# Transposed input from the host, layer norm folded into centered weights, and a new opening order in a four-stage block

## The chip, the cores and the metric

The kernel runs on one core of one Trainium2 chip. The metric is the device time of one execution in microseconds. Five engines of the core work side by side, each through its own queue of instructions, and meet through semaphores: TensorE (PE; its weight loads are shown apart as PEld), VectorE (DVE), ScalarE (ACT), GpSimd (POOL) and SyncE (SP), which here only starts DMAs.

## The reference

The input `x` has 4 batches of 512 tokens with 512 features. `_layernorm` has no weights: it subtracts the mean over the features and divides by the square root of the variance plus 1e-5.

```python
# _L0_attn_a_ref: a dense layer whose matrix is made here
attn = jnp.einsum('ds,td->st', w1, w2) * sparse_mask
y = jnp.einsum('bds,st->bdt', x, attn) + b2
return jax.nn.gelu(y, approximate=False)
# _L0_ffn_ref
dots = jax.nn.softmax(x @ centroids.T / TEMPERATURE, axis=-1)
hits = dots > THRESHOLD
query_sel, cluster_sel = jnp.any(hits, axis=1), jnp.any(hits, axis=0)
row_sel = cluster_sel[assignments]
dense = x @ weight.T + bias
out = jnp.where(query_sel[:, None] & row_sel[None, :], dense, 0)
...
x = x + _L0_attn_a_ref(_layernorm(x), w1, w2, b2, sparse_mask)      # stage 1
x = x + _L0_ffn_ref(_layernorm(x), weight, bias, centroids, assignments)   # stage 2
x = x + _L0_attn_b_ref(_layernorm(x), Wqkv, bqkv, Wo, bo)           # stage 3: one-head attention
x = x + _L0_ffn_ref(_layernorm(x), weight, bias, centroids, assignments)   # stage 4
```

All of it is float32. `cluster_sel` needs every token of every batch, so stages 2 and 4 each end in a point that all batches must reach.

## The kernel before

The 2048 tokens are 16 tiles of 128 tokens on the partitions (4 batches `b` of 4 tiles `t`, `n = 4b + t`), and `x_tok` holds them in on-chip memory throughout. A product that contracts over features needs its operands with the features on the partitions. So every normalized tile is transposed by TensorE in four 128x128 blocks, into one of four PSUM banks `t_bank` (line 1013). For accuracy each operand is split in two: ScalarE copies it rounded to a `_hi` part (line 719), VectorE subtracts that from the original to get a `_lo` part (line 813), and a product is the three matmuls hi·hi, lo·hi, hi·lo of each of the four 128-feature chunks, 12 matmuls in all (`products`, line 947), into one of four banks `m_bank`.

One tile of stage 1 passes these steps: VectorE's statistics (`stats`, lines 824 and 825), GpSimd's `rstd` and `nbias` (lines 650 to 652), ScalarE's `norm` into `xn_odd` (line 696), TensorE's transpose, the split, the product `y1` with the matrix `attn` and, as a thirteenth matmul, a row of ones times the split bias `b2` (line 951), ScalarE's Gelu straight from PSUM (line 734), and VectorE's residual sum into `x_tok` (step `x1`, line 850). Stage 2 normalizes the new `x_tok` into `xn_even` in the same way, transposes it, and makes two products: the cluster logits `cl2` for a whole batch (line 1048) and the dense `dn2` per tile. ScalarE copies `dn2` to `y_tok` (line 745) and GpSimd adds the bias (`bias_f`, line 661). The logits are transposed back (`tc2`); VectorE sums and subtracts their maximum (lines 905 to 908), ScalarE exponentiates in one instruction of 128x256 (line 784), and VectorE makes the selection (`prob2`, lines 914 to 924). Stage 4 is stage 2 again, with `x4`, `cl4`, `dn4`.

In the opening, `w2` is loaded in four column pieces and transposed by TensorE (16 blocks), `w1` is loaded in rows, and `attn` is built from 48 matmuls into the four `m_bank`s, masked by VectorE (line 836) and split (lines 723 and 840). The FFN weight arrives in the buffer that `w2` has left and is transposed between the tiles of batch 0.

The order is written out by hand. `schedule()` returns one list of steps; each engine walks that list and issues what is its own, so that a step's place in the list is its place in every engine's queue. In the loop over batches 1 to 3 it places the four `y1` products of batch `b` first and then `cl2` and four `dn2` of batch `b - 1`, with the transposes, splits and norms between them.

## Time and profile before

| | |
|---|---|
| median of 3 runs | 318.18 us (317.98 to 318.34) |
| span of the profiled execution | 317.0 us |
| TensorE busy | 285.5 us, 90% |
| VectorE busy | 232.8 us, 73% |
| ScalarE busy | 167.1 us, 53% |
| GpSimd busy | 162.3 us, 51% |

The span runs from the first to the last instruction of one profiled execution; what lies outside it is the rest of the device time. Engines are busy at the same time, so their shares don't add up. A share is a mean over stages. The granted clock of TensorE, given for a stretch, is 1.00 at 2.4 GHz and 0.50 at 1.2 GHz.

### The profile page before, as it was taken

The numbers are of one execution on the slowest core, as the hardware profiler recorded it, in microseconds if no ns is written. First come the engines' busy times: TensorE is split into PE (matmuls) and PEld (weight loads), VectorE is DVE, ScalarE is ACT, GpSimd is POOL, SyncE is SP. The second block draws the span as 40 slices with busy tenths as digits, with TensorE's granted clock in tenths as the row PEclk, the third lists the DMA queues.
The fourth block names the chain that finished last, engine by engine and source line by source line (L and its number), as shares of the span: only waits on it lengthen the run. The fifth ranks groups of instructions, "written<-read, shape, count | busy, mean of one in ns | idle before, by whom it ended". The sixth has DMA issues, their size and how long they took to land.

```text
span 317.0 us, 4389 instructions
## 1 busy us (share of the span) xinstructions
PE 285.5 (90%) x1444; PEld 232.4 (73%) x1444; DVE 232.8 (73%) x437; ACT 167.1 (53%) x287; POOL 162.3 (51%) x274
## 2 busy tenths in 40 slices
PE   2979999999999999977998999999997999998870
PEld 1758787788888888756886787888785777877650
DVE  1459889744956356985398868987889878788696
ACT  3527676775485448226376365656626466426210
POOL 2040647873784124338925398367953575127250
PEclk9997999999999999999999999999999999999995
DMA  6992910000000000000000000000000000000076
GB/s 217 290 342 67 353 42 4 0 0 2 0 0 2 0 0 1 2 1 0 2 0 0 2 1 2 1 0 1 2 0 0 2 0 0 3 0 1 0 284 246
DMA packets 9769, 14.82 MB, mean 47 GB/s; under 512 B 978, under 2 KB 3538, under 8 KB 9748
## 3 DMA queue, kind: packets, MB, share of 16 engines
q1 hardware_dynamic: 9748, 14.56, 13.4%
q8 instruction: 11, 0.18, 0.2%
q14 instruction: 10, 0.08, 0.1%
HBM read 10.36 MB, written 4.19 MB: 46 GB/s over the span
## 4 chain that ended last, share of the span: by engine, by line
PE 53%; DVE 24%; issue 6%; POOL 5%; ACT 5%; DMA 3%; SPq 2%; DVEq 0%; ACTq 0%; POOLq 0%
PE m_bank L947 40%; PE t_bank L1013 8%; PE m_bank L1048 4%; DMA x_tok<-in_L_attn_a_x 3%; DVE st L824 3%; DVE x_tok L864 3%; DVE y_tok L856 2%; POOL rstd L651 2%; DVE mx L888 2%; DVE w2t_lo L813 2%; DVE x_tok L869 1%; DVE odd_lo L813 1%; DVE even_lo L813 1%; POOL nbias L652 1%; DVE cl L916 1%
## 5 line engine op out<-in xcount | busy, mean ns | idle before, releaser
L650 POOL TENSOR_SCALAR ve<-mv 128x1 f32<-128x1 f32 x64 | 18.6, 290 | 102.0 <-DVE mv L825 99.8
L661 POOL TENSOR_TENSOR y_tok<-y_tok,bias_f 128x512 f32<-128x512 f32 x32 | 43.2, 1360 | 32.1 <-ACT y_tok L745 32.1
L824 DVE BATCH_NORM_STATS2 st<-x_tok 128x6 f32<-128x512 f32 x64 | 44.2, 691 | 6.6 <-DMA x_tok<-in_L_attn_a_x 4.9
L813 DVE TENSOR_TENSOR odd_lo<-t_bank,odd_hi 128x512 fp32r<-128x512 f32 x40 | 26.8, 684 | 22.8 <-ACT odd_hi L719 22.7
L651 POOL TENSOR_TENSOR rstd<-ve,half 128x1 f32<-128x1 f32 x64 | 37.6, 587 | 5.3
L947 PE MATMUL m_bank<-ffn_hi,even_hi 128*128 128x512 f32 x96 | 39.5, 412 | 0.0
L696 ACT ACTIVATE xn_odd<-x_tok,nbias,rstd 128x512 f32<-128x512 f32 x32 | 25.9, 813 | 22.6 <-POOL nbias L652 22.6
L947 PE MATMUL m_bank<-ffn_lo,even_hi 128*128 128x512 f32 x96 | 37.8, 393 | 0.0
L947 PE MATMUL m_bank<-ffn_hi,even_lo 128*128 128x512 f32 x96 | 37.4, 390 | 0.0
L745 ACT ACTIVATE y_tok<-m_bank 128x512 f32<-128x512 f32 x32 | 19.1, 595 | 33.6 <-PE m_bank L947 33.5
L696 ACT ACTIVATE xn_even<-x_tok,nbias,rstd 128x512 f32<-128x512 f32 x32 | 26.0, 812 | 19.6 <-POOL nbias L652 17.3
L947 PE MATMUL m_bank<-attn_hi,odd_hi 128*128 128x512 f32 x64 | 26.3, 411 | 0.0
L813 DVE TENSOR_TENSOR even_lo<-t_bank,even_hi 128x512 fp32r<-128x512 f32 x24 | 16.1, 682 | 12.9 <-ACT even_hi L719 12.8
L947 PE MATMUL m_bank<-attn_lo,odd_hi 128*128 128x512 f32 x64 | 25.1, 392 | 0.0
L947 PE MATMUL m_bank<-attn_hi,odd_lo 128*128 128x512 f32 x64 | 25.0, 390 | 0.0
L719 ACT ACTIVATE odd_hi<-t_bank 128x512 fp32r<-128x512 f32 x40 | 22.9, 591 | 3.6 <-PE t_bank L1013 3.6
L1013 PE MATMUL t_bank<-ident,xn_odd 128*128 128x128 f32 x128 | 19.0, 275 | 5.2 <-ACT xn_odd L696 4.0
L947 PE MATMUL m_bank<-odd_hi,wqkv_hi 128*128 128x512 f32 (+1 forms) x60 | 21.9, 365 | 1.0 <-DVE odd_lo L813 0.6
L1013 PEld LDWEIGHTS t_bank<-ident,xn_odd 128*128 128x128 f32 x128 | 14.8, 140 | 9.7 <-DVE odd_lo L813 4.4
L652 POOL TENSOR_SCALAR nbias<-mv,rstd 128x1 f32<-128x1 f32 x64 | 18.4, 287 | 6.3
L1013 PE MATMUL t_bank<-ident,w_raw 128*128 128x128 f32 x96 | 15.4, 299 | 6.2 <-DMA w_raw<-in_L_attn_a_w 6.2
L947 PEld LDWEIGHTS m_bank<-ffn_lo,even_hi 128*128 128x128 f32 x96 | 18.0, 188 | 4.0
(124 smaller groups left out, 714.5 us busy)
## 6 DMA issues: line engine op xcount, KB each, us to landing
x_tok<-in_L_attn_a_x SPq DMA_DIRECT2D x4, 1024.0 KB, 10.0
out<-x_tok SPq DMA_DIRECT2D x16, 256.0 KB, 2.1
w_raw<-in_L_attn_a_w SPq DMA_DIRECT2D x4, 256.0 KB, 4.9
...
y_tok<-in_L_attn_b_Wqkv SPq DMA_DIRECT2D x1, 768.0 KB, 4.7
...
```

The lines of the kernel that those rows point to most:

```text
L650: link(pool.tensor_scalar(ve[:, i:i + 1], mv[:, i, 1:2], EPS, None, ALU.add))
L651: link(pool.tensor_tensor(rstd[:, i:i + 1], ve[:, i:i + 1], half[:, :], ALU.pow))
L652: pool.tensor_scalar(nbias[:, i:i + 1], mv[:, i, 0:1], rstd[:, i:i + 1], -1.0, ALU.mult, ALU.mult).then_inc(rstd_done, 1)
L661: pool.tensor_tensor(y_tok[:, n, :], y_tok[:, n, :], bias_f[:, :], ALU.add).then_inc(biased, 1)
L696: act.activation(dst[:, t, :], x_tok[:, n, :], ACT.Identity, bias=nbias[:, i:i + 1], scale=rstd[:, i:i + 1]).then_inc(norm_done, 1)
L719: act.activation(split_of(what, b, t)[0], bank_view(what, t_bank[j % T_BANKS]), ACT.Copy).then_inc(t_hi, 1)
L745: act.activation(y_tok[:, n, :], bank[:, :], ACT.Copy).then_inc(m_act, 1)
L813: dve.tensor_tensor(lo, bank_view(what, t_bank[j % T_BANKS]), f32(hi), ALU.subtract).then_inc(t_free, 1)
L824: link(dve.bn_stats(st[:, at % 2, :], x_tok[:, n, :]))
L947: ins = pe.matmul(bank, a, w, start=(first and n == 0), stop=(last and n == count - 1))
L1013: ins = pe.transpose(bank[:, c * r:(c + 1) * r], blk, ident[0:r, 0:r])
L1048: ins = pe.matmul(bank[:, tokens], cen_hl[:, c, :], a[:, c, tokens], start=(c + h == 0), stop=(c == KC - 1 and h == 1))
```

## The change

**Data from the host.** The kernel gets a second copy of the input, `xt`, with the features before the tokens, and gets `w2` transposed. The four batches of `xt` (1 MB each) are loaded into `xn_odd` and the buffer `xt_other`, which takes the place of `xn_even`; `xt` of batch 1 goes where the FFN weight was, after that has been transposed. The 16 transposes of `w2` and the 64 of `x1` go. A new step `split_x` makes the hi part of `xt` on ScalarE and the lo part on GpSimd.

**Layer norm.** Subtracting the mean of the features of `x` gives the same product as subtracting from the weight its mean over those features. So the column mean of `attn` is made by four matmuls with a float32 matrix of 1/512 (`colmean`) and subtracted by VectorE (`center_attn`); the FFN weight and the centroids get their row means taken off (`center_f`, `center_c`: VectorE's statistics, GpSimd's negation, ScalarE's shift in place). Division by the deviation moves behind the product: in stage 1 a VectorE instruction (`scaled`) multiplies the bank by `rstd` and adds a broadcast `b2`, and Gelu then runs in place from on-chip memory; in stages 2 and 4 the copy of `dn` takes `rstd` as its scale, and the exponential runs as four instructions of 128x64, each with its own scale and bias. The norm steps of these stages, their `nbias`, the bias matmul and the subtraction of the maximum go. Stage 3 keeps its norm.

**Order.** The opening is reordered, the loop over batches 1 to 3 holds one transpose of `x2` for each `y1` tile, and the statistics of the next batch's stage 1 move from the `y1` tiles to the `dn2` tiles. `tc2` of batch 2 moves ahead of a `dn2`.

```diff
@@ schedule
     for c in range(KC):
-        step("T", "w2", 0, c)
+        step("w2", "", 0, c)
         step("w1", "", 0, c)
-        step("lo", "w2", 0, c)
-    for c in range(KC - 1):
         step("M", "attn", 0, c)
...
+    for c in range(KC):
+        step("center_f", "", 0, c)
+    step("center_c", "", 0, 0)
+    for t in range(TPB):
+        step("mask_attn", "", 0, t)
+    for t in range(TPB):
+        step("stats", 1, 0, t)
+    step("split_x", "", 0, 0)
+    step("split_x", "", 0, 1)
+    step("colmean", "", 0, 0)
+    step("T", "ffn", 0, 0)
+    step("T", "ffn", 0, 1)
+    step("center_attn", "", 0, 0)
...
         for t in range(TPB):
+            step("T", "x2", b - 1, t)
             step("M", "y1", b, t)
+            step("lo", "x2", b - 1, t)
+            if b == 1 or t:
+                residual("x1", 2, *divmod(b * TPB + t - 1, TPB))
+            step("scaled", "", b, t)
         step("M", "cl2", b - 1, 0)
...
             for t in range(TPB):
+                step("stats", 1, b + 1, t)
+                step("split_x", "", b + 1, t)
                 step("M", "dn2", b - 1, t)
@@ sync
+            sp.dma_start(ffn_raw[:, :, :], rows_of(ffn_d)).then_inc(ld["ffn"], 16)
+            sp.dma_start(cen_raw, cen_d).then_inc(ld["cen"], 16)
+            sp.dma_start(sparse, rows_of(sparse_d)).then_inc(ld["sparse"], 16)
+            load_x(0)
...
+            load_x(1)
+            sp.wait_ge(t_done, T_AT["ffn", 0, KC - 1] + 1)
+            load_xt(1)
@@ gpsimd
+                elif kind == "split_x":
+                    pool.wait_ge(x_hi_done, n + 1)
+                    pool.tensor_tensor(feat(odd_lo, t), feat(xt_raw[b % 2], t), f32(feat(odd_hi, t)),
+                                       ALU.subtract).then_inc(x_split, 1)
@@ scalar
-                        act.activation(y_tok[:, n, :], bank[:, :], ACT.Copy).then_inc(m_act, 1)
+                        act.activation(y_tok[:, n, :], bank[:, :], ACT.Identity,
+                                       scale=rstd[:, i:i + 1]).then_inc(m_act, 1)
...
-                    act.activation(ce[:, :, :], cl[:, :, :], ACT.Exp, scale=INV_TEMPERATURE).then_inc(c_exp, 1)
+                    for k in range(TPB):
+                        ins = act.activation(ce[:, k, :], cl[:, k, :], ACT.Exp, bias=ncmx[:, k:k + 1],
+                                             scale=rstd[:, i + k:i + k + 1])
+                    ins.then_inc(c_exp, 1)
@@ vector
+                elif kind == "scaled":
+                    dve.wait_ge(m_done, M_AT["y1", b, t] + 1)
+                    dve.wait_ge(rstd_done, STAT_AT[1, b, t] + 1)
+                    dve.scalar_tensor_tensor(out=gelu[:, n % 2, :], in0=m_bank[M_AT["y1", b, t] % M_BANKS][:, :],
+                                             scalar=rstd[:, n:n + 1], in1=b2[:, :], op0=ALU.mult,
+                                             op1=ALU.add).then_inc(m_dve, 1)
```

What this makes of VectorE's queue in the opening, from the last split of `w1` to the first splits of `attn` (`y_tok` is here the buffer of the mask and of `attn`). Before:

```order
L829 TENSOR_TENSOR even_lo<-y_tok,even_hi 128x512
L813 TENSOR_TENSOR w2t_lo<-t_bank,w2t_hi 128x512
L824 BN_STATS st<-x_tok 128x6
L825 BN_AGGR mv<-st 128x2
...
L813 TENSOR_TENSOR odd_lo<-t_bank,odd_hi 128x4x128 x2
L836 TENSOR_TENSOR y_tok<-m_bank,y_tok 128x512 x2
L840 TENSOR_TENSOR attn_lo<-y_tok,attn_hi 128x512
```

After (`fst` are the statistics of the FFN weight in `xt_other` and of the centroids in `lg`; `t_bank` holds the column mean):

```order
L850 TENSOR_TENSOR even_lo<-y_tok,even_hi 128x512 [waits w1_hi_done]
L882 BN_STATS fst<-xt_other 128x6 [waits ld_ffn]
...
L882 BN_STATS fst<-lg 64x6 [waits ld_cen]
L883 BN_AGGR fmv<-fst 64x2 [waits chain]
L857 TENSOR_TENSOR y_tok<-m_bank,y_tok 128x512 [waits m_done,ld_sparse]
L857 TENSOR_TENSOR y_tok<-m_bank,y_tok 128x512 [waits m_done] x3
L845 BN_STATS st<-x_tok 128x6 [waits ld_x0]
...
L871 TENSOR_TENSOR y_tok<-y_tok,t_bank 128x512 [waits t_done] x2
L861 TENSOR_TENSOR attn_lo<-y_tok,attn_hi 128x512 [waits attn_hi_done]
```

Five pairs of statistics of the weights now stand ahead of the four masks, and the four pairs of `x_tok` stand between the masks and the first centering.

GpSimd's queue at the same place, after the constants; `odd_lo` is what `split_x` writes:

```order
L652 TENSOR_SCALAR fmean<-fmv 128x1 [waits f_stats,consts]
L652 TENSOR_SCALAR fmean<-fmv 128x1 [waits f_stats] x3
L656 TENSOR_SCALAR fmean<-fmv 64x1 [waits f_stats]
L635 TENSOR_SCALAR ve<-mv 128x1 [waits stats_done]
L636 TENSOR_TENSOR rstd<-ve,half 128x1 [waits pchain]
...
L647 TENSOR_TENSOR odd_lo<-xn_odd,odd_hi 128x4x128 [waits x_hi_done] x4
```

The first lo parts of `xt` stand behind the four `rstd` of batch 0, which wait for VectorE's statistics.

VectorE's queue in one tile of the batch loop after the change:

```order
L832 TENSOR_TENSOR even_lo<-t_bank,even_hi 128x4x128
L898 TENSOR_TENSOR x_tok<-x_tok,y_tok 128x512
L845 BN_STATS st<-x_tok 128x6
L846 BN_AGGR mv<-st 128x2
L892 SCALAR_TENSOR_TENSOR y_tok<-m_bank,rstd,rows 128x512
```

The last of these is `scaled`; a second split, of `x1`, and the next batch's statistics stood in such tiles before.

## Rows read from the trace of the kernel before

**Rows 1.** The page's first part: busy us, share of the span, instructions

```profile
...
PE 285.5 (90%) x1444; PEld 232.4 (73%) x1444; DVE 232.8 (73%) x437; ACT 167.1 (53%) x287; POOL 162.3 (51%) x274
...
```

**Rows 2.** Windows by stage: us, busy us (count) per engine, granted clock, DMA share, GB/s

```profile
...
0.00:44.70 44.70, 36.32 (x168) 28.98 (x169) 27.52 (x51) 24.15 (x39) 13.88 (x42) 0.96 0.70 232
44.70:117.10 72.40, 71.90 (x360) 59.23 (x359) 47.36 (x94) 44.14 (x71) 41.76 (x79) 1.00 0.00 1
...
148.80:282.40 133.60, 128.50 (x673) 104.89 (x674) 105.41 (x202) 72.72 (x135) 77.84 (x113) 1.00 0.00 1
...
```

**Rows 3.** Chain of waits in batch 1's first matmul tiles: start us, length us, what

```profile
...
81.96 0.44 PE t_bank L1013 x4
82.40 2.77 PE m_bank L947 x12
85.17 0.23 PE m_bank L951
85.41 2.73 PE m_bank L947 x12
...
```

**Rows 4.** Timeline of TensorE: start us, us, instruction, idle before and its releaser

```profile
...
48.44 0.63 PE L1013 MATMUL t_bank<-ident,xn_odd 128*128 128x128 f32 x4 [0.50 <-ACT xn_odd L696]
...
```

**Rows 5.** Windows of the opening, columns as in Rows 2, last one GB/s

```profile
...
2.00:10.00 8.00, 3.77 (x14) 2.60 (x15) 2.53 (x4) 3.11 (x6) 0.60 (x4) 1.00 0.91 289
12.00:24.00 12.00, 9.94 (x44) 7.75 (x44) 5.79 (x12) 3.65 (x6) 4.08 (x11) 0.99 1.04 351
...
```

**Rows 6.** Windows around TensorE's pause in the opening; PEclk is the granted clock

```profile
...
20.20:23.70 3.50, 1.44 (x11) 1.21 (x11) 2.31 (x6) 2.25 (x4) 2.80 (x9) 1.00 1.04 351
23.70:27.10 3.40, 3.40 (x10) 2.63 (x9) 2.77 (x5) 2.94 (x5) 0.75 (x2) 0.50 0.40 151
...
```

**Rows 7.** Timeline of the opening, all engines

```profile
...
11.32 0.63 PE L947 MATMUL m_bank<-w2t_lo,even_hi 128*128 128x512 f32 x1
...
11.74 0.63 PE L947 MATMUL m_bank<-w2t_hi,even_hi 128*128 128x512 f32 x1
...
18.03 0.70 DVE L824 BATCH_NORM_STATS2 st<-x_tok 128x6 f32<-128x512 f32 x1 [4.88 <-DMA x_tok<-in_L_attn_a_x]
...
```

**Rows 8.** DMA issues: KB each, median us from issue to landing

```profile
...
y_tok<-in_L_attn_b_Wqkv SPq DMA_DIRECT2D x1, 768.0 KB, 4.7
...
```

**Rows 9.** Groups by line and shape: busy us, mean ns of one, idle before

```profile
...
L824 DVE BATCH_NORM_STATS2 st<-x_tok 128x6 f32<-128x512 f32 x64 | 44.2, 691 | 6.6 <-DMA x_tok<-in_L_attn_a_x 4.9
L661 POOL TENSOR_TENSOR y_tok<-y_tok,bias_f 128x512 f32<-128x512 f32 x32 | 43.2, 1360 | 32.1 <-ACT y_tok L745 32.1
...
L651 POOL TENSOR_TENSOR rstd<-ve,half 128x1 f32<-128x1 f32 x64 | 37.6, 587 | 5.3
...
L696 ACT ACTIVATE xn_even<-x_tok,nbias,rstd 128x512 f32<-128x512 f32 x32 | 26.0, 812 | 19.6 <-POOL nbias L652 17.3 <-PE t_bank L1013 2.3
...
L876 DVE SCALAR_TENSOR_TENSOR attn_hi<-m_bank,bqkv,attn_hi 128x512 fp32r<-128x512 f32 x8 | 6.0, 744 | 3.3 <-ACT attn_hi L760 3.3
...
L784 ACT ACTIVATE ce<-cl 128x256 f32<-128x256 f32 x8 | 3.3, 418 | 15.3 <-DVE cl L908 15.2
...
L686 ACT ACTIVATE even_hi<-y_tok 128x512 fp32r<-128x512 f32 x4 | 2.5, 623 | 0.0
...
```

**Rows 10.** Timeline: VectorE at 134.07 and its neighbour in time on GpSimd

```profile
...
133.94 1.28 POOL L661 TENSOR_TENSOR y_tok<-y_tok,bias_f 128x512 f32<-128x512 f32 x1 [4.73 <-ACT y_tok L745]
134.07 1.44 DVE L916 TENSOR_TENSOR cl<-ce,crec 128x256 f32<-128x256 f32 x1
...
```

**Rows 11.** Timeline of VectorE: the same instruction undisturbed

```profile
...
277.50 0.42 DVE L916 TENSOR_TENSOR cl<-ce,crec 128x256 f32<-128x256 f32 x1
...
```

**Rows 12.** Timeline of VectorE: the wait for the cluster exponential

```profile
...
276.84 0.42 DVE L914 TENSOR_REDUCE csum<-ce 128x4 f32<-128x256 f32 x1 [0.49 <-ACT ce L784]
...
```

**Rows 13.** Timeline of TensorE in stages 3 and 4: idle before, and its releaser

```profile
...
241.96 0.70 PE L947 MATMUL m_bank<-w2t_hi,attn_lo 128*128 128x512 f32 x2 [1.67 <-DVE w2t_lo L813]
...
286.15 0.63 PE L1013 MATMUL t_bank<-ident,xn_even 128*128 128x128 f32 x4 [0.43 <-ACT xn_even L696]
...
```

More of the change, by code:

```diff
@@ L116, in schedule @@
+    step("split_x", "", 1, 0)
+    residual("x1", 2, 0, 2)
+    step("scaled", "", 0, 3)
+    for t in range(1, TPB):
+        step("stats", 1, 1, t)
+        step("split_x", "", 1, t)
+    step("onehot", "", 0, 0)
     for b in range(1, NB):
         for t in range(TPB):
-            jobs = []
-            if b == 1 and t < 2:
-                jobs.append(("x1", 1, t + 2))
-            if b == 1 or t + 1 < TPB:
-                jobs.append(("x2", b - 1, t + (b > 1)))
-            for job in jobs:
-                step("T", *job)
@@ L938, in _, with products @@
         def _(pe):
-            pe.wait_ge(consts, 7)
-            def products(bank, pairs, bias=None, first=True, last=True):
-                count = 3 * len(pairs) + (bias is not None)
+            pe.wait_ge(consts, 6)
+            def products(bank, pairs, first=True, last=True):
+                count = 3 * len(pairs)
                 n = 0
@@ L948, in products @@
                         n += 1
-                if bias is not None:
-                    pe.wait_ge(bias_split, 1)
-                    ins = pe.matmul(bank, ones[:, :], bias[:, :], start=False, stop=True)
                 return ins
@@ L1033, in _ @@
                     if what == "y1":
[L1034 to L1041 removed]
+                        pe.wait_ge(x_split, n + 1)
+                        ins = products(bank, [((odd_hi[:, c, cols], odd_lo[:, c, cols]),
+                                               (attn_hi[:, c, :], attn_lo[:, c, :])) for c in range(KC)])
                     elif what in ("cl2", "cl4"):
```

367 lines of the change are left out of this document (200 added, 167 removed).

## The prediction

> **What bounds the kernel now.** I read the page's first part, which has TensorE busy for 90% of the span [rows 1], and then windows by stage, to see where that holds [rows 2]. From 44.7 to 117.1 us, from batch 1's first `y1` to batch 3's last, TensorE is busy for 71.9 of 72.4 us while VectorE is at 65%: here an instruction taken from TensorE is time. Stages 3 and 4 up to 282.4 are nearly as dense (128.5 of 133.6). The opening is not: 36.3 of 44.7, with a pause and a slow clock in it. The two turning points (117 to 149, and after 282) are chains through all engines. So I count TensorE's instructions for the middle stretch, and follow waits for the rest.
>
> **The batch loop, 44.7 to 117.1.** The chain of waits shows the unit prices [rows 3]: a product of 12 matmuls takes 2.73 to 2.77 us, the bias matmul 0.23, the four transposes of a tile 0.44. All 12 bias matmuls of batches 1 to 3 go: 12 x 0.235 = 2.8 us. Of the `x1` transposes 9 tiles fall in this stretch (the last of batch 1, four each of batches 2 and 3): 9 x 0.44 = 4.0. The 11 tiles of `x2` stay 11. The one idle gap, 0.50 us behind an `x1` norm [rows 4], goes too. Together **-7.3 us**, if nothing else becomes late. Next in line is VectorE. One `y1` tile now holds the lo part and the `x1` sum (0.69 each, from the row of 0.686 to 0.691 for this size), statistics of about 0.9 with their short second instruction, and `scaled`, for which the nearest row is the 0.744 of an operation of its kind out of PSUM [rows 9]: 3.0 us beside TensorE's 2.77 + 0.44 = 3.2. The next batch's statistics lie in the `dn2` tiles, where VectorE has room. GpSimd does one `rstd` chain per `y1` tile. In the four `dn2` tiles it has four `rstd` (0.9 each), four lo parts at 1.36, the price of an addition of the same size [rows 9], four bias additions at 1.36 and some late splits: about 18 us against 13 of TensorE. But batch `b+1`'s lo parts are wanted at 3.2 us intervals only after those 13, so the last one has 22 us. I take no stall.
>
> **The opening.** I ask when batch 1's first `y1` starts; before it is 44.7.
> - Loads. Between 2 and 10 us, with `w2` in column pieces, 289 GB/s arrived, from 12 to 24 us, with whole rows, 351 [rows 5]. With rows throughout, the first 2.1 MB should be there by 8.5 to 10 us, the FFN weight (1.05 MB, 3 us) by 12 to 13, centroids and mask by 15 to 16.5, `x` of batch 0 by 18 to 19.5 and the first half of its `xt` by 19.5 to 21.
> - `attn`. Its matmuls start near 5 us instead of 10.3, since no transpose stands ahead. They run at first 0.42 us apart [rows 7], at the lower clock; at 0.23 the 48 end near 18 us.
> - VectorE's queue is the longer chain. Five pairs of weight statistics (0.9 each) from 12.5 end at 17, four masks (0.7) at 20, four statistics of `x` at 23.5. Only then come centering and splits: eight instructions of 0.69, to 29.
> - GpSimd's lo parts of the first two tiles stand behind the fourth `rstd` (near 24.5) and take 1.36 each, so `y1` of tiles 0 and 1 starts near 27.3. TensorE has then been idle for some 5 us. After idle times of 1.4 and 0.7 us the granted clock went to 0.50 for 3.4 us even though the engine was at work again [rows 6]. So I take 3.9 us at 0.42 (9 matmuls) and 15 at 0.23: end at 34.6. The column mean hides in the wait for VectorE, at the 0.23 of a 512-column matmul and even at four times that.
> - The transposes of the last FFN tiles end at 35.5 and only then release the load of batch 1's `xt`. Wo and Wqkv (1 MB too) took 4.7 us plus 0.4 of issue [rows 8]; with 5.0, hi 0.62 and lo 1.36 `y1` of batch 1 can start at 42.4. TensorE's own chain (two products, small transposes) ends at 41.7.
>
> So **-2.3 us**, and -5.2 to +2.5 between all these at their best and worst.
>
> **Middle turning point.** The logits' exponential becomes four instructions. From the 0.418 of 256 columns and the 0.623 of 512 [rows 9] one of 64 takes 0.27 us; the norm's 0.812 against 0.623 puts two pointer operands at 0.19, so 0.45 each: four take 1.8 us one by one, and I take 1.5, with some overlap (an estimate), instead of 0.42, and 0.3 less on VectorE ahead of it, since one 128x4 instruction replaces the subtraction. Net +0.75 where VectorE waits for it. At batch 3's clusters it does (0.5 us before, as at [rows 12]); the earlier `tc2` gives back some 0.5. **+0.2** (-0.4 to +1.0).
>
> **Stages 3 and 4.** Stage 4's norms go from ScalarE and from TensorE's path: the gap of 0.43 at 286.15 [rows 13] and two of 0.2 like it, **-0.8**. The longer exponential lies ahead of the probabilities' transposes: the gap at 241.96, which ends on the split of these [rows 13], grows by 0.75; at 276.84 VectorE already waits for it [rows 12] and Wo's product comes 0.5 later: **+1.2**. For batch 0's I count nothing, as TensorE has work in hand there. The scale operand on the `dn` copies (0.1 each) is hidden by bank rotation. At the end TensorE's last `dn4` products cover the longer exponential (0.85 us of room). Together **+0.4**, between -1.0 and +2.5.
>
> **Sum.** -2.3 - 7.3 + 0.2 + 0.4 = -9.0 us on the span of 317.0, so 308.0; the median of the runs lies 1.2 above the span, so **309.2 us**.
>
> **Rivals.**
> - *The opening gains nothing or loses.* If the loads come no earlier, GpSimd and VectorE slow each other in the splits, and the clock stays low for longer, `y1` of batch 1 starts at 46 to 48 instead of 42.4: 313 to 315. For it: three serial chains end on VectorE's queue, which became longer by nine pairs of statistics ahead of the centering.
> - *Row loads are no faster than column loads.* By the rates of [rows 5] the pieces may have differed only because queues were filling. Then all loads stand 1 to 1.5 us later and the time is 310.4. The Trainium skill has this rule: "DMA: Bandwidth & Descriptors", section Specifications, asks for at least 512 B per transfer for line rate, which the column pieces just reach. By that rule the layout change buys no bandwidth; the trace's 289 against 351 speaks against it, weakly.
> - *The opening does better.* With loads at the early ends and a clock that rises sooner, batch 1 starts at 39.5: 306.3.
> - *Slower than before: VectorE becomes the bound of the batch loop.* A VectorE instruction with two inputs in on-chip memory took 1.44 us beside a GpSimd addition [rows 10] and 0.42 alone [rows 11]. `split_x` puts 16 such GpSimd instructions more into the loop. If they spilled over into the `y1` tiles and each hit both the `x1` sum and its neighbour, a tile would cost VectorE 3.0 + 1.2 = 4.2 us, 1.0 over TensorE's 3.2; 12 tiles lose 12 us, and the time is 321. It decides from 0.75 us over, 3.95 per tile. Against it: `scaled`, the lo part and the statistics don't read two such inputs, and GpSimd's lo parts are queued in the `dn2` tiles. The Trainium skill ("GPSIMD Engine Reference", section 1. Specifications) names this contention, for VectorE instructions with two SBUF inputs.
> - *The change doesn't reach the bound.* TensorE's removed work turns into idle, because Gelu, which now has VectorE before and after it, holds something up. The batch loop is then as long as before: 318.18 - 2.3 + 0.6 = 316.5. Against: four banks, and no transpose of `x2` is wanted within a tile of its sum.
>
> **Chances.** Forecast, 307.5 to 311.5 without the row-load case: 0.45. Row loads no faster: 0.10. Opening loses: 0.19. Opening better, to 305.5: 0.13. Not reaching the bound: 0.05, of which 0.02 near no change. VectorE bound and slower: 0.05. What is left, 0.03, is a larger gain. The range of 305.5 to 314.0 takes in all but the worst of the lost opening and the last two rivals. A measurement of this kernel tells 0.2% (0.6 us) from no change, so: faster 0.92, same 0.03, slower 0.05.
>
> **What would show it.** In the profile of the changed kernel: no line of a bias matmul, and TensorE dense from batch 1 to batch 3 in about 65 us instead of 72.4; its first product of batch 1 at 42.4; a granted clock of 0.50 after the first centered split; VectorE's four statistics of batch 0 between masks and centering; the four exponentials within 1.5 us; the gap before the third batch's attention product near 2.4 us. I am wrong if TensorE shows idle times in the batch loop that end on VectorE, or if the load of batch 1's `xt` lands well after 41.

## The result: slower, 328.5 us instead of 318.3

| | before | after |
|---|---|---|
| median | 318.26 us (317.98 to 320.28, 4 runs) | 328.47 us (327.76 to 330.27, 4 runs) |
| span of the profiled execution | 317.0 us | 327.0 us |
| TensorE | 285.5 us busy | 282.6 us busy |
| VectorE | 232.8 us busy | 243.7 us busy |

The ratio is 1.032, with a 95% interval of 1.028 to 1.037. Medians here and below are over all runs, while the ratios leave out the few runs more than 1.5% above the fastest of their kernel (one each of e4, e10 and, beside e9 to e12, the kernel before). The forecast was 309.2 us, in a range of 305.5 to 314.0, with 5% for slower. The first part of the page of the changed kernel stands against [rows 1]: 88 instructions fewer on TensorE, and ScalarE has lost 20 us.

```profile
PE 282.6 (86%) x1356; PEld 228.5 (70%) x1356; DVE 243.7 (75%) x450; ACT 146.8 (45%) x266; POOL 166.2 (51%) x246
```

The windows by stage (us, then busy us and count for PE, PEld, DVE, ACT, POOL, then granted clock, DMA share, GB/s) are cut at batch 1's first `y1`, at the end of batch 3's last `y1`, at the first `q` and behind the last `Wo` product:

```profile
0.00:47.89 47.89, 32.26 (x128) 24.35 (x129) 32.55 (x59) 21.00 (x33) 15.07 (x36) 0.90 0.68 228
47.89:120.59 72.70, 68.63 (x308) 55.48 (x308) 50.88 (x94) 32.02 (x56) 49.71 (x74) 0.95 0.15 54
120.59:153.98 33.39, 27.02 (x126) 21.87 (x127) 25.22 (x49) 16.14 (x29) 12.29 (x23) 0.95 0.00 0
153.98:291.70 137.72, 131.31 (x685) 108.00 (x686) 105.28 (x202) 69.53 (x135) 76.44 (x103) 0.99 0.00 1
```

Against [rows 2] the opening is 3.2 us longer (47.89 for 44.70) and the batch loop, which was to lose 7.3, is 0.3 longer. It has 52 matmuls fewer, but it is idle for 4.1 us and has a granted clock of 0.95 instead of 1.00. The rest, from 117.1 in the one and 120.6 in the other to the end, adds 6.5 us.

**The batch loop: a ring of waits.** TensorE's rows with a wait, from batch 1's first `y1` to the `cl2` of batches 0, 1 and 2 (the last at 122; start us, us, instruction, idle before and who ended it):

```profile
47.89 0.76 PE L997 MATMUL m_bank<-attn_hi,odd_hi 128*128 128x512 f32 x1 [5.48 <-POOL odd_lo L647]
63.99 0.47 PE L1125 MATMUL m_bank<-even_hi,cen_hl 128*128 128x512 f32 x1 [1.55 <-DVE even_lo L832]
92.74 0.47 PE L1125 MATMUL m_bank<-even_hi,cen_hl 128*128 128x512 f32 x1 [2.51 <-DVE even_lo L832]
...
122.47 0.47 PE L1125 MATMUL m_bank<-even_hi,cen_hl 128*128 128x512 f32 x1 [1.89 <-DVE even_lo L832]
```

`cl2` needs the lo parts of all four `x2` tiles, so a VectorE that falls behind in the four `y1` tiles is billed there. VectorE and ScalarE in one such tile:

```profile
54.96 0.69 DVE L832 TENSOR_TENSOR even_lo<-t_bank,even_hi 128x512 fp32r<-128x512 f32 x1 [1.18 <-ACT even_hi L715]
55.57 0.68 DVE L898 TENSOR_TENSOR x_tok<-x_tok,y_tok 128x512 f32<-128x512 f32 x1
56.29 0.69 DVE L845 BATCH_NORM_STATS2 st<-x_tok 128x6 f32<-128x512 f32 x1
57.02 0.18 DVE L846 BATCH_NORM_AGGREGATE mv<-st 128x2 f32<-128x6 f32 x1
57.12 0.75 DVE L892 SCALAR_TENSOR_TENSOR y_tok<-m_bank,rstd,rows 128x512 f32<-128x512 f32 x1
59.06 0.69 DVE L832 TENSOR_TENSOR even_lo<-t_bank,even_hi 128x512 fp32r<-128x512 f32 x1 [1.18 <-ACT even_hi L715]
```

```profile
57.91 0.63 ACT L735 ACTIVATE y_tok<-y_tok 128x512 f32<-128x512 f32 x1 [2.98 <-DVE y_tok L892]
58.45 0.58 ACT L715 ACTIVATE even_hi<-t_bank 128x512 fp32r<-128x512 f32 x1
```

From one lo part to the next (54.96 to 59.06) it is 4.10 us, of which VectorE works 2.9 and waits 1.18. Neither engine is full: ScalarE waited 2.98. Lo waits for hi; hi stands in ScalarE's queue behind Gelu; Gelu waits for `scaled`; `scaled` stands in VectorE's queue behind the previous lo part, sum and statistics. Only the queue's order ties hi to Gelu: the transpose that hi reads had run at 55.89 to 56.49.

**The half clock.** TensorE was granted 1.2 GHz though it was fully busy: at the start of batch 1, behind the wait of 5.48 us, until about 52, then for 3.4 us each behind the waits at 92.74 and 122.47, and again from 154.5 behind a chain of shorter ones (columns as in the windows above; the clock is the 0.50 behind the five engines). Its matmuls are then 0.43 us apart instead of 0.23, so that such a stretch of 3.4 us costs about 1.6 (an estimate from these spacings).

```profile
48.00:52.00 4.00, 4.00 (x10) 3.13 (x11) 3.90 (x9) 2.11 (x5) 3.82 (x7) 0.50 1.05 394
93.10:96.50 3.40, 3.40 (x10) 2.62 (x9) 2.60 (x6) 0.91 (x2) 0.79 (x2) 0.50 0.00 0
123.80:127.20 3.40, 3.40 (x16) 3.00 (x15) 2.64 (x6) 2.12 (x4) 1.01 (x3) 0.50 0.00 0
154.50:157.90 3.40, 3.40 (x18) 3.40 (x17) 0.69 (x1) 1.31 (x3) 3.40 (x4) 0.51 0.02 5
```

**The opening** kept to the forecast up to 42 us: `y1` of tiles 0 and 1 started at 27.19 (forecast 27.3), and TensorE's own work ended at 42.4 (forecast 41.7). Batch 1's `xt`, issued at 35.93 and 5.2 us under way, landed at 41.2 to 41.6, about 1 us behind the 40.5 that the forecast implies. Then `y1` of batch 1 started at 47.89 instead of 42.4:

```profile
42.25 0.75 DVE L892 SCALAR_TENSOR_TENSOR y_tok<-m_bank,rstd,rows 128x512 f32<-128x512 f32 x1
...
43.03 0.63 ACT L735 ACTIVATE y_tok<-y_tok 128x512 f32<-128x512 f32 x1 [3.98 <-DVE y_tok L892]
43.57 0.36 ACT L715 ACTIVATE cen_hl<-t_bank 128x256 fp32r<-128x256 f32 x1
43.83 0.62 ACT L721 ACTIVATE odd_hi<-xt_other 128x512 fp32r<-128x512 f32 x1
43.97 0.42 DVE L832 TENSOR_TENSOR cen_hl<-t_bank,cen_hl 128x256 fp32r<-128x256 f32 x1 [0.97 <-ACT cen_hl L715]
...
44.31 0.68 DVE L845 BATCH_NORM_STATS2 st<-x_tok 128x6 f32<-128x512 f32 x1
...
45.95 0.57 POOL L636 TENSOR_TENSOR rstd<-ve,half 128x1 f32<-128x1 f32 x1
46.48 1.26 POOL L647 TENSOR_TENSOR odd_lo<-xt_other,odd_hi 128x512 fp32r<-128x512 f32 x1
```

The hi part waited behind a Gelu, some 2.4 us from the landing of the load, and GpSimd's lo part, 2.0 us from the end of hi, behind an `rstd` whose statistics on VectorE stood behind all of that.

### The profile page after: what moved, and what is told of

Same layout as the page of the kernel before. It is cut to its first block, busy times and chain, and to the rows that moved or that the text cites. A ratio compares the mean times of both kernels' runs of the same rounds, so it can differ in the third digit from the quotient of the medians.

```text
span 327.0 us, 4206 instructions
## 1 busy us (share of the span) xinstructions
PE 282.6 (86%) x1356; PEld 228.5 (70%) x1356; DVE 243.7 (75%) x450; ACT 146.8 (45%) x266; POOL 166.2 (51%) x246
## 4 chain that ended last, share of the span: by engine, by line
PE 43%; DVE 30%; issue 9%; ACT 8%; POOL 5%; DMA 3%; SPq 1%; DVEq 0%; ACTq 0%
PE m_bank L997 34%; DVE st L845 5%; PE t_bank L1060 4%; PE m_bank L1125 4%; DMA xt_other<-in_L_ffn_weight 3%; DVE x_tok L898 3%; DVE y_tok L892 2%; ACT even_hi L715 2%; DVE even_lo L832 2%; DVE x_tok L912 2%; DVE w2t_lo L832 2%; DVE y_tok L904 2%; DVE x_tok L917 2%; POOL rstd L636 2%; DVE mx L936 2%
## 5 line engine op out<-in xcount | busy, mean ns | idle before, releaser
L635 POOL TENSOR_SCALAR ve<-mv 128x1 f32<-128x1 f32 x64 | 16.6, 259 | 99.5 <-DVE mv L846 99.1
L759 ACT ACTIVATE y_tok<-m_bank,rstd 128x512 f32<-128x512 f32 x32 | 21.9, 684 | 44.5 <-PE m_bank L997 44.4
L735 ACT ACTIVATE y_tok<-y_tok 128x512 f32<-128x512 f32 x16 | 10.0, 630 | 42.1 <-DVE y_tok L892 42.1
L832 DVE TENSOR_TENSOR odd_lo<-t_bank,odd_hi 128x512 fp32r<-128x512 f32 x24 | 15.8, 681 | 9.6 <-ACT odd_hi L715 9.5
L997 PEld LDWEIGHTS m_bank<-attn_hi,odd_hi 128*128 128x128 f32 x64 | 13.1, 205 | 13.0 <-DVE y_tok L892 5.7
L997 PE MATMUL m_bank<-odd_lo,wqkv_hi 128*128 128x512 f32 (+1 forms) x60 | 21.6, 361 | 0.0
L997 PE MATMUL m_bank<-odd_hi,wqkv_lo 128*128 128x512 f32 (+1 forms) x60 | 21.6, 360 | 0.0
L674 POOL TENSOR_TENSOR x_tok<-x_tok,bo 128x512 f32<-128x512 f32 x16 | 20.7, 1298 | 0.0
L997 PEld LDWEIGHTS m_bank<-ffn_hi,even_lo 128*128 128x128 f32 x96 | 18.2, 190 | 3.3
L997 PEld LDWEIGHTS m_bank<-ffn_hi,even_hi 128*128 128x128 f32 x96 | 18.2, 190 | 3.2
```

The lines of the kernel that those rows point to most:

```text
L635: link(pool.tensor_scalar(ve[:, i:i + 1], mv[:, i, 1:2], EPS, None, ALU.add))
L674: pool.tensor_tensor(x_tok[:, n, :], x_tok[:, n, :], bo[:, :], ALU.add).then_inc(bo_added, 1)
L735: act.activation(gelu[:, n % 2, :], gelu[:, n % 2, :], ACT.Gelu).then_inc(gelu_done, 1)
L759: act.activation(y_tok[:, n, :], bank[:, :], ACT.Identity, scale=rstd[:, i:i + 1]).then_inc(m_act, 1)
L832: dve.tensor_tensor(lo, bank_view(what, t_bank[j % T_BANKS]), f32(hi), ALU.subtract).then_inc(t_free, 1)
L997: ins = pe.matmul(bank, a, w, start=(first and n == 0), stop=(last and n == count - 1))
```

## The experiments

Theory A: the loss is in the order of the queues between VectorE and ScalarE, which makes rings and chains of waits, and in the half clock behind TensorE's waits. Theory B: VectorE has too much to do, GpSimd's use of the memory port included. C: the longer exponential costs more than forecast. The median of before drifted by a few tenths between the sessions, so the ratio to it is the better number. The clock is part of the noise: the mean granted clock of e10's ten executions, for one, went from 0.964 to 0.987, and their times from 319.9 to 314.4 us. A profile shows one execution.

| run | median us | before beside it | ratio (95%) |
|---|---|---|---|
| e1 Gelu behind hi | 321.03 | 319.08 | 1.006 (1.003 to 1.009) |
| e2 no GpSimd lo | 323.52 | 319.08 | 1.016 (1.010 to 1.021) |
| e3 split first | 328.42 | 319.08 | 1.031 (1.024 to 1.039) |
| e4 one exponential | 323.61 | 319.08 | 1.012 (1.003 to 1.021) |
| e5 e1 + e3 | 319.39 | 319.92 | 0.999 (0.996 to 1.002) |
| e6 opening relieved | 315.05 | 319.92 | 0.985 (0.981 to 0.990) |
| e7 e6 + row sums | 313.88 | 319.92 | 0.981 (0.977 to 0.986) |
| e8 Gelu from the bank | 317.94 | 319.92 | 0.995 (0.991 to 0.998) |
| e9 dense opening | 316.91 | 319.42 | 0.994 (0.990 to 0.997) |
| e10 e9 + row sums | 317.15 | 319.42 | 0.992 (0.988 to 0.995) |
| e11 halves only | 319.38 | 319.42 | 1.001 (0.999 to 1.004) |
| e12 e10, ring put back | 326.07 | 319.42 | 1.022 (1.018 to 1.026) |
| e13 chain shortened | 311.79 | 318.48 | 0.978 (0.972 to 0.984) |
| e14 e13, table early | 312.30 | 318.48 | 0.980 (0.974 to 0.986) |
| e15 waits filled | 325.51 | 318.48 | 1.022 (1.014 to 1.030) |
| e16 e14 without its flaw | 312.28 | 319.76 | 0.976 (0.971 to 0.982) |
| e17 turning points filled | 311.26 | 319.76 | 0.973 (0.968 to 0.978) |
| e18 e13, no GpSimd lo | 311.12 | 319.76 | 0.971 (0.963 to 0.979) |

### The ring: e1, e2, e8, e12

e1 makes Gelu a step of its own and issues it behind the next tile's hi part; the other engines keep their order:

```diff
             step("T", "x2", b - 1, t)
+            if t:
+                step("gelu", "", b, t - 1)
             step("M", "y1", b, t)
...
             step("scaled", "", b, t)
+        step("gelu", "", b, TPB - 1)
         step("M", "cl2", b - 1, 0)
```

> Only ScalarE's order in the batch loop changes: the Gelu of tile t-1 goes behind the hi part of the next x2 tile instead of ahead of it. Theory A, a ring of waits (scaled, Gelu, hi, lo, x1, statistics, scaled) makes a y1 tile 4.1 us: the ring is cut, VectorE's period falls to 3.2 us, the gaps of 1.55, 2.51 and 1.89 us ahead of cl2 go with most of the half clock behind them, and the time falls by 6 to 10 us, to 318.5 to 322.5. Theory B, VectorE simply has too much work in such a tile (GpSimd slowing it included): period stays near 4 us and the time within 1 us of 328.5.

It gained 7.4 us by the medians and 8.4 by the ratios (1.032 to 1.006). VectorE in a tile of the same batch:

```profile
57.13 0.68 DVE L839 TENSOR_TENSOR even_lo<-t_bank,even_hi 128x512 fp32r<-128x512 f32 x1
57.91 0.69 DVE L905 TENSOR_TENSOR x_tok<-x_tok,y_tok 128x512 f32<-128x512 f32 x1
58.64 0.69 DVE L852 BATCH_NORM_STATS2 st<-x_tok 128x6 f32<-128x512 f32 x1
59.37 0.18 DVE L853 BATCH_NORM_AGGREGATE mv<-st 128x2 f32<-128x6 f32 x1
59.48 0.75 DVE L899 SCALAR_TENSOR_TENSOR y_tok<-m_bank,rstd,rows 128x512 f32<-128x512 f32 x1
60.14 0.68 DVE L839 TENSOR_TENSOR even_lo<-t_bank,even_hi 128x512 fp32r<-128x512 f32 x1
```

The period is 3.01 us: the same five instructions, with no wait. Beside GpSimd's work it is 3.5 (lo parts at 83.92 and 87.44). Of the three gaps ahead of `cl2` (1.55, 2.51, 1.89) one of 0.44 is left. The batch loop, cut as in the windows above, took 66.8 us (47.51 to 114.34) instead of 72.7. The half clock from 47.5 to 51.2 and that at the first `q` stayed, and one more came at 136.5.

e2 cuts `split_x` on GpSimd to `feat(odd_lo, t)[:, :, 0:4]` for batches 1 to 3:

> Leaves work out: for batches 1 to 3 GpSimd makes only 4 of the 128 columns of each lo part of xt (0.3 us instead of 1.3), so VectorE has less GpSimd traffic beside it. Theory A: period of a y1 tile stays at 4.0 to 4.1 us in the batch loop, and only the first product of batch 1 starts about 1 us earlier; time 326.5 to 328. Theory B, GpSimd's port contention: period falls towards 3.2 us, time 320 to 322.

Against theory B the ring keeps its period and its 1.19 us of wait (81.10 to 85.20):

```profile
81.10 0.69 DVE L833 TENSOR_TENSOR even_lo<-t_bank,even_hi 128x512 fp32r<-128x512 f32 x1 [1.19 <-ACT even_hi L716]
...
85.20 0.69 DVE L833 TENSOR_TENSOR even_lo<-t_bank,even_hi 128x512 fp32r<-128x512 f32 x1 [1.19 <-ACT even_hi L716]
```

But the time fell by 5 us (5.3 by the ratios), to 323.5, between what A (326.5 to 328) and B (320 to 322) had expected: it started batch 1 1.9 us earlier, the second gap was 1.42 instead of 2.51, and the half clocks behind the second and third gap were absent. Where the changed kernel's ring is the bound, a disturbance of one VectorE instruction is billed in full, and it can bring the half clock with it.

e8 undoes the part of the change that made the ring: Gelu reads the bank and takes `rstd` as its scale, with no pass of VectorE.

```diff
-                    act.wait_ge(*m_freed(M_AT["y1", b, t]))
-                    act.activation(gelu[:, n % 2, :], gelu[:, n % 2, :], ACT.Gelu).then_inc(gelu_done, 1)
+                    act.wait_ge(m_done, m + 1)
+                    act.activation(gelu[:, n % 2, :], m_bank[m % M_BANKS][:, :], ACT.Gelu,
+                                   scale=rstd[:, n:n + 1]).then_inc(m_act, 1)
```

> Leaves work out: b2 is not added and VectorE's scaling pass is gone; Gelu reads the bank itself with rstd as its scale. The order of the steps is that of the changed kernel. Theory A: Gelu waits for TensorE alone, the ring is gone as in e1 and VectorE has 0.75 us less per tile: tiles of 3.2 us, no gap ahead of cl2, first y1 of batch 1 at 45.5 to 47, 317.5 to 320.5 us. Theory B (load, contention): the same direction, but gaps ahead of cl2 stay in part.

All gaps ahead of `cl2` went, with the order of the steps as in the changed kernel. It is `scaled` on VectorE that couples the two queues; e8 by itself would also fit theory B, since it takes 0.75 us per tile off VectorE, which e1 does not. e12 is the other direction, put into a kernel whose opening is relieved (e10, below):

> e10 with Gelu ahead of the hi part again in the batch loop, as in the changed kernel: the ring put back where everything else is relieved. Theory A: tiles of 4.1 us on VectorE, cl2 gaps of 2 to 3.5 us in each of the three batches and half a clock behind them: 8 to 12 us slower than e10. If the ring had only mattered because VectorE was late from the opening: less than 4 us.

```profile
60.27 0.76 PE L1132 MATMUL m_bank<-even_hi,cen_hl 128*128 128x512 f32 x1 [7.30 <-DVE even_lo L840]
```

8.9 us slower than e10 (9.8 by the ratios), with VectorE's period again 4.10 (lo parts at 51.24, 55.34 and 59.43); the gaps came as 7.30, 1.77 and 1.51 us, not as 2 to 3.5 each. The ring costs 7 to 9 us by the medians, 8 to 10 by the ratios, shown in both directions, the half clock behind its gaps included.

### The opening: e3, e5, e11, e6, e9, e10, e13, e14, e16

e3 moves one step of the changed kernel:

```diff
+    step("split_x", "", 1, 0)
     step("scaled", "", 0, 2)
...
     step("stats", 1, 1, 0)
-    step("split_x", "", 1, 0)
```

> One step moved: the split of batch 1's first xt tile goes ahead of the scaling of tile (0,2) and of the statistics of (1,0), on ScalarE and on GpSimd. If the queue orders hold back batch 1's first y1 (start 47.9), it starts at 43.8 (load 41.8, hi 0.6, lo 1.3), the gap of 5.5 us becomes 1.4, and the time falls by 2 to 4 us to 324.5 to 326.5; less than 2 if the ring of waits behind it takes the gain back. If it was the load or the low clock instead, the start stays past 46.

```profile
44.91 0.47 PE L997 MATMUL m_bank<-attn_hi,odd_hi 128*128 128x512 f32 x1 [2.25 <-POOL odd_lo L647]
...
63.99 0.76 PE L1125 MATMUL m_bank<-even_hi,cen_hl 128*128 128x512 f32 x1 [3.80 <-DVE even_lo L832]
```

TensorE started 3.0 us earlier, and `cl2` at 63.99, to the hundredth where it was, with 328.42 us. So the chain that ends the opening is VectorE's; starting TensorE earlier only moved the idle time, and behind the longer wait the clock was 0.50 from 64 to 69.5. e5 has both edits:

> The reordered Gelu (e1) and the earlier split of batch 1's first tile (e3) together. Theory A says that the ring of waits took back what e3 gained (start 44.9 instead of 47.9, but a gap of 3.8 us ahead of cl2): with the ring cut, the gain of e3 stays, and the time is 2 to 3 us under that of e1, 318 to 319. If VectorE's work after the opening is a bound of its own, less than 1 us.

It came 1.6 us under e1 by the medians and 2.3 by the ratios. But `cl2` moved only from 61.69 to 61.08, with a gap of 1.18, and batch 2's `cl2` from 114.34 to 114.20, so the gain did not stay in the opening as A said: VectorE is late by itself there. Most of the difference of the two profiles (2.5 us) lies behind that, where the edit has no part and e1 had two stretches of half clock (136.5 and 146.8) in which e5 ran at 1.00. e11 adds to e5 the load of batch 1's `xt` in two halves, the first as soon as the second FFN tile is transposed:

```diff
+            sp.wait_ge(t_done, T_AT["ffn", 0, 1] + 1)
+            sp.dma_start(xt_raw[1][:, :, early], rows_of(xt_d[1][:, early])).then_inc(ld["xt1"], 16)
             sp.wait_ge(t_done, T_AT["ffn", 0, KC - 1] + 1)
-            load_xt(1)
+            sp.dma_start(xt_raw[1][:, :, late], rows_of(xt_d[1][:, late])).then_inc(ld["xt1_late"], 16)
```

> Of e6's four edits of the opening only the load of batch 1's xt in halves, with its first split ahead of the scaling of (0,2); VectorE's statistics of batch 1 stay behind the opening. If the load was the only thing late, first y1 of batch 1 at 43 and a time near 316. By what e5 showed (a gap of 1.2 us ahead of cl2 returned as soon as y1 started earlier) VectorE is late by itself: cl2 of batch 0 stays past 60 and the time within 1.5 us of e5's 319.4.

Nothing (`cl2` at 60.66, 319.38 us): the load was not what was late. e6 also takes work out of VectorE's way: the statistics of batch 1 go to where it had nothing to do (31 to 34 us), the one-hot table to a `dn2` tile, and GpSimd splits tiles (0,0) and (0,1) ahead of batch 0's `rstd`. Which of these three makes the gain was not tested apart.

> e1, and the opening relieved of its waits: batch 1's xt in two halves, the first loaded once the second FFN tile is transposed; the statistics of batch 1's stage 1 on VectorE while it has nothing to do at 31 to 34 us; GpSimd's first two splits ahead of batch 0's rstd; the one-hot table in a dn2 tile of batch 0. First y1 at 25 to 26, first y1 of batch 1 at 40.5 to 42 without a gap, cl2 of batch 0 at 54 to 56 instead of 61.7, and 313 to 316 us. If VectorE stays behind TensorE after the opening, cl2 comes past 58.

`cl2` came at 55.35, 6.3 us earlier than in e1, and the median fell by 6.0. e9 removed the next visible wait of TensorE, 2.35 us on the lo part of tile (1,0), by placing that split ahead of `residual("x1", 2, 0, 0)`:

> e6, whose first y1 of batch 1 stood 2.4 us behind GpSimd: the lo part of tile (1,0) was queued behind the rstd of x1(0,1). Here the splits of tiles (1,0) and (1,1) stand ahead of them. First y1 of batch 1 at 37.6 to 38.5 without a gap, TensorE at its full clock there, cl2 of batch 0 at 50.8 to 52 instead of 55.3, and 3 to 4.5 us less than e6: 310.5 to 312. If VectorE's pile of work after the opening is the bound, cl2 comes past 54 and the gain is under 1.5 us.

> e9 with the exponentials that add up their rows (as e7 stands to e6): another 1 to 1.5 us, 309.3 to 311.

Both missed. `y1` of batch 1 started at 39.0 without a gap, and the time rose by 2 us. In the profile `cl2` of batch 0 came 1.1 us later than in e6 (56.42 for 55.35) and batch 1's 3.9 later (86.45 for 82.58): the difference is the half clock behind the long gap, 0.50 from 57 to 62. The rows of e9, TensorE's first:

```profile
56.42 0.77 PE L1135 MATMUL m_bank<-even_hi,cen_hl 128*128 128x512 f32 x1 [3.86 <-DVE even_lo L842]
```

```profile
42.94 0.75 DVE L902 SCALAR_TENSOR_TENSOR y_tok<-m_bank,rstd,rows 128x512 f32<-128x512 f32 x1
45.91 0.69 DVE L842 TENSOR_TENSOR even_lo<-t_bank,even_hi 128x512 fp32r<-128x512 f32 x1 [2.22 <-ACT even_hi L725]
```

```profile
43.73 0.63 ACT L745 ACTIVATE y_tok<-y_tok 128x512 f32<-128x512 f32 x1 [3.08 <-DVE y_tok L902]
44.26 1.14 ACT L731 ACTIVATE odd_hi<-xt_other 128x512 fp32r<-128x512 f32 x2
45.30 1.06 ACT L725 ACTIVATE even_hi<-t_bank 128x512 fp32r<-128x512 f32 x2
```

The ring again, once: VectorE waits 2.22 us for a hi part that stands behind a Gelu that waits for VectorE. e13 takes out this link, and leaves TensorE's start alone:

```diff
     step("M", "y1", 0, 3)
-    residual("x1", 2, 0, 2)
+    step("T", "x2", 0, 0)
+    step("lo", "x2", 0, 0)
     step("scaled", "", 0, 3)
     step("gelu", "", 0, 3)
+    residual("x1", 2, 0, 2)
```

> e10 started y1 of batch 1 without a gap and was no faster: VectorE waited 2.2 us for the hi part of x2(0,0), which stood on ScalarE behind a Gelu that stood behind VectorE. Here the transpose and split of x2(0,0) stand ahead of the scaling of (0,3). If VectorE's chain of waits, not TensorE's start, sets cl2 of batch 0, it moves from 56.8 to 53 to 54, its gap from 3.85 to about 1.2, the half clock behind it goes, and the time is 4 to 5 us under e10's: 312 to 313.5. Otherwise it stays near 317.

```profile
54.21 0.47 PE L1138 MATMUL m_bank<-even_hi,cen_hl 128*128 128x512 f32 x1 [0.84 <-DVE even_lo L846]
```

`cl2` moved from 56.81 to 54.21, its half clock went, and the time is 311.79, 5.4 us under e10 (4.2 by the ratios): 2.2% faster than before (1.6 to 2.8). It keeps e10's row sums. e14 brings Gelu's table in early by a Gelu of one column:

> e13, and a Gelu of one column while ScalarE has nothing to do (about 28 us), so that the 1.28 us load of its table no longer stands ahead of the first Gelu. The first x1 on VectorE comes 1.2 us earlier and cl2 of batch 0 at 52 to 52.5, which is when TensorE gets there: another 1 us, 311 to 312.5. No gain if the table is loaded again at the first real Gelu.

The table was not loaded again and the first `x1` came 1.1 us earlier, but the wait that I had put ahead of ScalarE's first copy made TensorE start at 6.1 instead of 4.8 us. e16 puts it right:

> e14 again with its side effect taken away (ScalarE waited for GpSimd's constants ahead of its first copy, and TensorE started at 6.1 instead of 4.8 us); the wait now stands at the one-column Gelu. Against e13: cl2 of batch 0 1.0 to 1.5 us earlier, at 52.8 to 53.3, and 0.5 to 1.5 us less time, 310.5 to 311.5. If the table's place does not matter, the same as e13.

```profile
33.91 1.28 ACT L749 ACT_TABLE_LOAD   x1
```

`cl2` was at 52.67 instead of 54.21 (in part because its first `y1` pair fell at a faster clock), yet the ratio of 0.976 can't be told from e13's 0.978, and the expected gain is not shown. The row is e13's: ScalarE's next Gelu starts at 35.20, right behind the load. The Trainium skill ("ScalarE: Activation LUTs", section What ACT_TABLE_LOAD costs) gives 1283 ns for the load, with which the trace agrees, and about 1380 ns more for a drain; no drain shows here, and the measurement decides.

### The exponential: e4, e7

e4 replaces the four exponentials by one:

```diff
-                    for k in range(TPB):
-                        ins = act.activation(ce[:, k, :], cl[:, k, :], ACT.Exp, bias=ncmx[:, k:k + 1],
-                                             scale=rstd[:, i + k:i + k + 1])
+                    ins = act.activation(ce[:, :, :], cl[:, :, :], ACT.Exp, bias=ncmx[:, 0:1],
+                                         scale=rstd[:, i:i + 1])
```

> Leaves work out: the exponential of the cluster logits is one instruction of 128x256 with the scale and shift of the first tile for all four, instead of four of 128x64. It takes 0.4 instead of 1.44 us. If the long exponential lies on the path at the middle turning point, twice in stages 3 and 4 and at the end, the time falls by 2 to 4 us, to 324.5 to 326.5. If it is hidden, by less than 1.

The time fell by 4.9 us by the medians and 6.5 by the ratios (whose interval is wide, 1.003 to 1.021), but the profile gives the exponential only part of it. The last `Wo` product and the last mask, changed kernel first, then e4:

```profile
288.86 0.70 PE L997 MATMUL m_bank<-wo_hi,attn_lo 128*128 128x512 f32 x2 [0.97 <-DVE attn_lo L932]
...
311.21 0.47 PE L1171 MATMUL m_bank<-onehot,csel 128*128 128x512 f32 x1 [1.19 <-DVE csel L984]
```

```profile
285.21 0.70 PE L996 MATMUL m_bank<-wo_hi,attn_lo 128*128 128x512 f32 x2 [0.22 <-DVE attn_lo L931]
...
307.72 0.47 PE L1170 MATMUL m_bank<-onehot,csel 128*128 128x512 f32 x1 [0.67 <-ACT y_tok L759]
```

From the first `q` (153.98, in e4 152.47) to the last mask e4 is 2.0 us shorter, and 0.8 from there to the end: 2.8 us, what the clock did there included (a stretch at half clock lay behind the last mask in the one, at 299.5 to 303 in the other). At the end the exponential costs more than its length, since a short VectorE instruction comes to lie beside GpSimd's bias addition. In the changed kernel `qsel` took 1.15 us, in e4 and before 0.17:

```profile
307.05 1.57 POOL L663 TENSOR_TENSOR y_tok<-y_tok,bias_f 128x512 f32<-128x512 f32 x1 [5.59 <-ACT y_tok L759]
...
307.49 1.15 DVE L969 TENSOR_SCALAR qsel<-crec 128x4 f32<-128x4 f32 x1
```

The other 1.5 us of its span were gained before the first `q`, 1.3 of them before batch 1's first `y1`, where the edit has no part. Four exponentials took 1.44 us on ScalarE (0.43 each), one of 128x256 with the same operands 0.60, and 0.42 with none [rows 9].

e7 lets the exponentials add up their rows, `accum_out=csum[:, k:k + 1]`, and drops the sum on VectorE:

> e6, and the four exponentials of the cluster logits also add up their rows (the sums that VectorE made from their output in 0.42 us on the same path). 0.4 us less at the middle turning point, at the third attention product, at the last Wo and at the last selection: 1.5 to 2 us less than e6 if adding up costs ScalarE nothing; no gain if it costs 0.1 or more per exponential.

The rows refute the reason: each exponential is followed by a read of the sum, and VectorE waits 1.88 us instead of 1.5.

```profile
269.83 0.44 ACT L810 ACTIVATE ce<-cl,ncmx,rstd 128x64 f32<-128x64 f32 x1 [2.23 <-DVE ncmx L967]
270.18 0.19 ACT L810 ACTIVATION_READ_ACCUMULATOR ce<-cl,ncmx,rstd 128x1 f32 x1
```

About 0.1 us of the 0.42 is left; the 1.2 us between e6 and e7 (0.985 and 0.981, with intervals that overlap) were not this, since e10 shows no gain over e9 clear of the noise.

### The clock and the port: e15, e17, e18

e15 lets TensorE repeat a product, whose result is overwritten, in the waits of the changed kernel:

```diff
+                        if what == "cl2" and b < NB - 1:
+                            for _ in range((5, 9, 6)[b]):
+                                pe.matmul(bank, attn_hi[:, 0, 0:P], attn_hi[:, 0, :], start=True, stop=True)
```

> The changed kernel with 16, 5, 9 and 6 matmuls whose result is thrown away in TensorE's waits ahead of batch 1's first y1 and of the three cl2, so that TensorE works on while it waits. The waits stay as long; what changes is only the granted clock behind them. If the half clock (3.4 us long at 93, 124 and 154 us, and 7 us from 45) is part of the loss, TensorE runs at 1.00 there, and the time falls by 3 to 5 us to 323.5 to 325.5; if the ring of waits covers it, by less than 1.

```profile
94.00:97.00 3.00, 3.00 (x16) 2.48 (x15) 2.23 (x5) 1.74 (x4) 0.77 (x3) 1.00 0.00 0
```

The clock behind the filled waits is 1.00, though TensorE was still idle for 2.46 us ahead of the first `cl2`, and 3 us of the loss are back, at the lower edge of what was expected; the intervals (1.028 to 1.037 and 1.014 to 1.030) overlap slightly. The first `q` still ran at 0.50. So the half clock is a cost of its own, beside the waits that it follows. e17 does the same in e16's waits at the two turning points:

> e16 with TensorE's waits at the two turning points and ahead of q filled with matmuls whose result is thrown away (1 to 4 in each wait of 0.6 to 1.2 us). If those waits bring on the half clock behind them (q of batch 0, the last four dn4), TensorE stays at 1.00 there and the time falls by 1 to 3 us; if not, it stays or rises by up to 1 us for matmuls that overrun a wait.

The intervals of the two ratios (0.973 and 0.976) overlap, and in the profiles of both `q` ran at 1.00 in any case. The last `dn4` ran at 0.50 from 293.8 to 297 in e16 and at 1.00 in e17, but also at 1.00 in e13, without filling, and e17 had other stretches at 0.50 (25.2 and 234). So whether the waits at the turning points cost clock stays open. e18 repeats e2 on e13:

> Leaves work out: e13 with GpSimd's lo parts of batches 1 to 3 cut to 4 of 128 columns, as in e2. In e2 this gave 5 us. If that was VectorE slowed through a shared port in a kernel where its ring was the bound, little is left to gain now: 0 to 1.5 us less than e13, the cl2 gaps of 0.85 and 0.94 us (each behind an x1 of 1.4 us) gone. If GpSimd's own queue was the cause, again 3 us or more.

From batch 0's `cl2` to batch 2's it took 52.3 us instead of 53.5, and the second gap (0.94) was gone; the first was 1.14 instead of 0.84. That is the price of GpSimd's lo parts there once the ring is cut, port and queue together: about 1.2 us. Over the whole kernel it is 0.7 us by the medians and 2.3 by the ratios, whose intervals overlap. The `x1` sum, with two inputs in on-chip memory, beside GpSimd's work, in the changed kernel:

```profile
83.17 2.99 POOL L663 TENSOR_TENSOR y_tok<-y_tok,bias_f 128x512 f32<-128x512 f32 x2
```

```profile
83.22 1.79 DVE L898 TENSOR_TENSOR x_tok<-x_tok,y_tok 128x512 f32<-128x512 f32 x1
```

It takes 0.68 alone. The Trainium skill ("GPSIMD Engine Reference", section 1. Specifications) says that VectorE and GpSimd contend when a VectorE instruction has two SBUF inputs; the trace agrees.

## Why the prediction was wrong, point by point

- **The batch loop, -7.3 us: measured +0.3.** The sum on TensorE was right: bias matmuls and `x1` transposes went (52 matmuls fewer; the forecast counted 48, with nine tiles of transposes). VectorE's 3.0 us per undisturbed tile was right too, as e1's 3.01 shows. The step that failed is "I take no stall", drawn from comparing 3.0 with 3.2: it compares the loads of two engines and leaves out the way through a third. Through ScalarE's queue the same five instructions need 4.10. Of the missed 7.6 us, 4.1 are the ring's first two gaps and some 1.6 the half clock behind the second; cutting the ring (e1) gave back 5.9 in this stretch. The other 2 are the half clock in batch 1's first product, which came behind the opening's wait of 5.48 us and stayed in e1. The sign that the prediction gave for being wrong, idle times in the batch loop that end on VectorE, is what the profile shows.
- **The rival that had it** was "Gelu, which now has VectorE before and after it, holds something up". It got 0.05 and a price of zero gain, since I asked whether a bank or a transpose was wanted within a tile, and not what stands behind Gelu in ScalarE's own queue. That was the hi part of the next tile.
- **The rival of VectorE as the bound** (0.05) had the right row: 4 us per tile on VectorE, 1.0 over TensorE. Its mechanism was the smaller part. e2 kept the ring at 4.10 without GpSimd's lo parts. But in the changed kernel taking GpSimd's lo parts out gave 5 us, because the ring bills each disturbance in full and the half clock went with it; with the ring cut (e18) it is 1.2 us in the loop.
- **The opening, -2.3: measured +3.2.** Up to the first two `y1` everything was within half a microsecond (27.19 for 27.3, their end at 34.9 for 34.6). The failed step is the last, "with 5.0, hi 0.62 and lo 1.36": it takes both parts as ready to run when the load lands. Hi stood behind a Gelu for some 2.4 us and lo behind an `rstd` for 2.0; the load, about 1 us late, makes the rest of the 5.5. And the question itself was badly put, because e3 started TensorE 3.0 us earlier than the changed kernel and e9 1.6 us earlier than e6, both for nothing: what ends the opening is VectorE's chain up to `cl2` of batch 0, not TensorE's first `y1`. One reading went beyond its rows, without effect on the time: the first matmuls do run 0.42 us apart, but that this is "at the lower clock" rests on the spacing alone; the trace of before gives 1.00 as the granted clock there, from 10 to 13 us as in [rows 5].
- **Middle, +0.2.** From the end of batch 3's last `y1` to the first mask it took 24.2 us instead of 20.7 (137.75 less 117.10 before). The ring's tail (the gap of 1.89 ahead of `cl2`, some 1.6 of half clock behind it) makes most of it; the exponential alone was rightly sized, 1.44 for my 1.5.
- **Stages 3 and 4, +0.4: measured +2.9** (first `q` at 153.98 for 146.88). The first `q` ran at half clock (0.9 us). For two places of the exponential I had 1.2: against before, TensorE is 0.8 us later from batch 0's `Wo` to the third attention product (the gap itself grew only from 1.67 to 1.75, not to 2.4; 0.59 stand ahead of a transpose before it) and 0.45 to the last `Wo`, so that was right. The norms gave back 0.5 for my 0.8. The failed step is the end, which I had covered by the last `dn4` products and put at nothing: the last mask waits 1.19 and comes another 1.5 us later, through the exponential and the slow `qsel` behind it.
- **Row loads** came near the forecast: 311 GB/s between 2 and 10 us and 364 from 12 to 24, against 289 and 351 [rows 5]. Whether the layout made the first difference, 8%, was not tested apart.

The change is good once its queues are put in order: e13 keeps all of it and runs at 0.978 of before. That this is close to the forecast (0.972) is in part luck: e13's opening is shorter than forecast (`y1` of batch 1 at 39.5 for 42.4), by steps that the forecast knew nothing of, and its batch loop is longer (68.2 us for some 65).
